# Attention on one core: where turned row maxima and diagonal masks stand in a hand-written order

## The chip, the cores and the metric

The kernel runs on one core of one Trainium2 chip. The metric is device time in microseconds from start to end of one execution. Three executions of the kernel before took 2019.26, 2020.14 and 2020.37 us; the median is 2020.14 us.

## What is computed

A transformer layer on 2048 tokens of width 512: a layer norm, causal attention with 16 heads of 32, and a gated feed-forward part, both added to the input.

```python
xn = _layernorm(x, axis=-1)
# attention
qkv = jnp.einsum('bsh,oh->bso', hidden_states, w_qkv)   # 16 heads of 32
scores = jnp.einsum('bhqd,bhkd->bhqk', q, k) * scale
scores = jnp.where(causal, scores, jnp.finfo(scores.dtype).min)
probs = jax.nn.softmax(scores, axis=-1)
attn = jnp.einsum('bhqk,bhkd->bhqd', probs, v)
# feed-forward
gelu = jnp.tanh(0.7978845608028654 * (gate + 0.044715 * gate ** 3)) * gate * 0.5 + gate * 0.5
inter = gelu * up
x = x + attn @ w_o.T + inter @ Wd.T
```

## The kernel before, in words

Three stages follow each other: `norm_and_project` (norm, q, k and v to scratch memory), `attention`, and `project_and_feed_forward`. The change touches `attention` alone.

Attention handles the heads in 8 pairs (`PAIRS`). For a pair there are two kinds of scores. The **units** (`scores`, L680) are query-major: 128 queries by up to 512 keys into one of four banks of `p_s`; they serve only to find each query's maximum. VectorE reduces each unit to one column of `max_part` (L604, or L600 with the mask added where the unit touches the diagonal). When all units of a chunk of 512 queries are reduced, `join_parts` (L611) joins them, GpSimd splits the maxima into three bf16 parts (`split`, L504 to L514), and TensorE **turns** them: `turn_max` (L690) multiplies `max_cols` by an identity and puts the maxima as rows into a bank of `p_s`. ScalarE copies that bank into spare rows of `q_stack` (`max_row`, L540). There they take part in the second kind of scores, so that the maximum is already subtracted when these come out. Each head of a chunk has one turned maximum: 64 in all, for 8 pairs, 4 chunks and 2 heads.

The **scores_t** (L706) are key-major: 128 keys by up to 512 queries into one of three banks of `p_st`. On the diagonal a second matmul, `mask_k` by the identity (L712, 128 columns, bf16), adds the mask into the same bank. ScalarE takes the exponential into `e_sb` (`exps`, L551), and the **products** (`product_v`, L727) multiply it by v into `p_o`, with a row of sums. `copy_out` (L562) takes `p_o` to SBUF when a chunk is done.

A step is one block of 128 keys of one chunk; a pair has 40 steps (chunks of 4, 8, 12 and 16), and the last four of each chunk are its diagonal. Every step has two pieces, one per head. The order of the work is written out by hand in groups of 4 steps (`GS`), numbered by `k` from 0 to 79: group `k` issues the eight pieces of scores_t of the next group's steps (`LEAD` = 4), the units that `units_of(k)` assigns to it in eight parts (`some_units`), and the products of its own four steps. Since the chunks are multiples of four steps, a group's scores_t are all on the diagonal or none is. Eight units is the normal measure; the first groups take up to `UNITS_FIRST` = 12, until they are `UNITS_AHEAD` = 56 ahead.

`TURNS[k]` lists the turned maxima of group `k`. For pairs 1 to 7 they are turned one group before the scores_t that need them (`TURN_LEAD` = 1), for the last two chunks of pair 0 in the same group (`FIRST_LEAD` = 0); those of chunks 0 and 1 of pair 0 come before group 0. `ring` (L327) is the order in which units and turned maxima take the four banks of `p_s`, and `bank_free` (L665) waits for the reader of the bank's former content: VectorE for a unit, ScalarE's `max_row` for a turned maximum.

TensorE opens a group so:

```python
for t in TURNS[k]:
    turn_max(*t)
for n in range(3):
    scores_t(x + n)
some_units(0, 8)
some_units(1, 8)
scores_t(x + 3)
```

and closes it with `scores_t(x + 7)`, four `product_v` and `some_units(7, 8)`. ScalarE takes in a group three exps, the copies of the turned maxima, `copy_out` of a finished chunk, and five exps (L573 to L585); for pair 0 the copies come first.

Of the kernel before, what the change touches and what calls it, by code (L numbers as in the profile page):

```python
# [29 lines left out]
P = 128  # L30
# [232 lines left out]
def attention(nc, qk_scratch, v_scratch, sum_scratch, rsum_scratch, wo_t, wo_sb, attn_t):  # L263
# [14 lines left out]
    UNITS_FIRST = 12  # L278
    UNITS_AHEAD = 56
    TURN_LEAD = 1  # L280
    FIRST_LEAD = 0
# [22 lines left out]
    for k in range(NG):  # L304
        done = min(NUNIT, max(done + UNITS_GROUP, min(done + UNITS_FIRST, UNITS_GROUP * (k + 1) + UNITS_AHEAD)))
        unit_end.append(done)

    def units_of(k):
        return list(range(unit_end[k - 1] if k else FIRST, unit_end[k]))
# [4 lines left out]
    for p in range(PAIRS):  # L314
        for r in range(TC):
            last = p * NU + UNITS_TO[r]
            BATCHES[-1 if last <= FIRST else next(k for k in range(NG) if unit_end[k] >= last)].append((p, r))
            wanted = (p * NS + CHUNK_START[r] - LEAD) // GS
            for a in range(2):
                TURNS[max(-1, -1 if p == 0 and r < 2 else wanted - (FIRST_LEAD if p == 0 else TURN_LEAD))].append((p, r, a))  # L320
# [7 lines left out]
    for k in range(NG):  # L328
        ring += TURNS[k] + units_of(k)
# [6 lines left out]
    with ExitStack() as ctx:  # L336
# [200 lines left out]
        def _(act):  # L537
# [35 lines left out]
            for k in range(NG):  # L573
                x = (GS * k + LEAD) * PIECES
                for t in TURNS[k]:
                    if t[0] == 0:
                        max_row(*t)
                for n in range(3):
                    exps(x + n)
                for t in TURNS[k]:  # L580
                    if t[0] > 0:
                        max_row(*t)
                copy_out_before(k)
                for n in range(3, GS * PIECES):
                    exps(x + n)  # L585

        @block.vector
        def _(dve):
# [62 lines left out]
            for k in range(NG):  # L651
# [5 lines left out]
                for p_, r in BATCHES[k]:  # L657
                    join_parts(p_, r)
# [5 lines left out]
        def _(pe):  # L664
# [29 lines left out]
            def scores_t(x):  # L694

                g, heads = piece(x)
# [4 lines left out]
                if kt == 0:  # L701
                    pe.wait_ge(max_rows, turn_index[p, qc, heads[-1]] + 1)
                if x >= ST_BUFS:
                    pe.wait_ge(exp_done, x - ST_BUFS + 1)
                for n, a in enumerate(heads):
                    last = nc.tensor.matmul(p_st[:, x % ST_BUFS, n, 0:W - q0],  # L706
                                            k_stack[p % PB][a][:, kt * P:(kt + 1) * P],
                                            q_stack[p % PB][a][:, qc * W + q0:(qc + 1) * W], start=True,
                                            stop=not DIAG[s])
                if DIAG[s]:  # L710
                    for n, a in enumerate(heads):
                        last = nc.tensor.matmul(p_st[:, x % ST_BUFS, n, 0:P], ident[:, :], mask_k[:, :], start=False,  # L712
                                                stop=True)
                last.then_inc(st_ready, 1)
# [23 lines left out]
            for x in range(LEAD * PIECES):  # L738
                scores_t(x)
            pe.wait_ge(o_cleared, 1)  # L740
            for k in range(NG):
# [6 lines left out]

                for t in TURNS[k]:
                    turn_max(*t)  # L750
                for n in range(3):
                    scores_t(x + n)
                some_units(0, 8)
                some_units(1, 8)
                scores_t(x + 3)
                some_units(2, 8)
                scores_t(x + 4)
                some_units(3, 8)
                scores_t(x + 5)
                some_units(4, 8)  # L760
                some_units(5, 8)
                scores_t(x + 6)
                some_units(6, 8)
                scores_t(x + 7)
# [395 lines left out]
```

## Time and profile before

| | us |
|---|---|
| median of three runs | 2020.14 |
| the profiled execution, its own time | 2020.79 |
| span of its profile | 2018.9 |
| TensorE matmuls busy | 1882.5 (93% of the span) |
| VectorE busy | 1090.2 (54%) |
| ScalarE busy | 693.9 (34%) |
| GpSimd busy | 310.7 (15%) |
| mean granted TensorE clock | 0.984 of full speed |

The profile gives for each engine the time in which it worked; matmuls are pipelined and their ends are modelled, so that a busy TensorE can still be waiting a little between matmuls, and the starts tell more than the durations. PE is TensorE's matmuls, PEld its weight loads, DVE is VectorE, ACT ScalarE, POOL GpSimd. L706 is line 706 of the kernel. "idle 0.86 <-ACT q_stack L540" says that an engine stood still for 0.86 us and that ACT's instruction of line 540 released it.

### The profile page before, as it was taken

How to read it: one execution, taken by the hardware profiler on the slowest of the kernel's cores; microseconds unless marked ns; L12 is line 12 of the kernel's file. 1: busy time of each engine (PE TensorE's matmuls, PEld its weight loads, DVE VectorE, ACT ScalarE, POOL GpSimd, SP SyncE). 2: the span in 40 equal slices, each digit the busy share in tenths (PEclk: the TensorE clock that was granted, in tenths of full speed). 3: DMA queues.
4: the chain of work that ended last, by engine and by line, in shares of the span. 5: the costliest groups of instructions: out<-in, count | busy, mean ns of one | idle time of the engine just before them, and what ended most of it. 6: DMA issues, size and time to landing. Idle time of an engine off the chain costs nothing.

```text
span 2018.9 us, 23894 instructions
## 1 busy us (share of the span) xinstructions
PE 1882.5 (93%) x8448; PEld 1325.6 (66%) x8448; DVE 1090.2 (54%) x1706; ACT 693.9 (34%) x1112; POOL 310.7 (15%) x339
## 2 busy tenths in 40 slices
PE   2997799999999999989999999999999999999998
PEld 2785444444444444336787778777877787778776
DVE  7220566565565655643565556555655565556553
ACT  2221345455555555511222222222222222222231
POOL 0002200100101111101212221222122212221221
PEclk9999699999999999999999999999999999999999
DMA  3654603223134040052100110111011101110002
GB/s 146 237 190 119 124 6 79 62 49 81 40 69 82 17 93 6 11 198 63 32 7 26 31 31 5 27 31 31 2 29 31 31 1 30 31 31 0 0 1 83
DMA packets 88857, 109.31 MB, mean 54 GB/s; under 512 B 44248, under 2 KB 60632, under 8 KB 85008
## 3 DMA queue, kind: packets, MB, share of 16 engines
q1 hardware_dynamic: 88784, 108.39, 19.9%
q8 instruction: 40, 0.66, 0.1%
q14 instruction: 33, 0.27, 0.1%
HBM read 75.09 MB, written 29.59 MB: 52 GB/s over the span
## 4 chain that ended last, share of the span: by engine, by line
DVE 21%; ACT 12%; POOL 10%; issue 7%; PE 6%; POOLq 0%; DVEq 0%; ACTq 0%
POOL poly L958 7%; DVE acc L1031 5%; DVE inter L1011 4%; DVE inter L1015 4%; ACT inter L930 3%; POOL poly L955 3%; ACT gate L926 3%; ACT poly L927 3%; DVE weight L1000 3%; ACT i_hi L933 2%; DVE magnitude L994 2%; DVE pair L987 2%; PE p_out L1096 1%; DVE high L991 1%; PE p_gate L1096 1%
## 5 line engine op out<-in xcount | busy, mean ns | idle before, releaser
L551 ACT ACTIVATE e_sb<-p_st 128x512 f32<-128x512 f32 (+3 forms) x640 | 297.3, 548 | 279.8 <-PE p_st L706 145.8
L604 DVE TENSOR_REDUCE max_part<-p_s 128x1 f32<-128x512 f32 x384 | 241.7, 684 | 108.7 <-PE p_s L680 108.5
L680 PE MATMUL p_s<-k_stack,q_stack 96*128 96x512 f32 (+3 forms) x640 | 232.8, 413 | 42.8 <-ACT q_stack L540 21.0
L1011 DVE SCALAR_TENSOR_TENSOR inter<-inter,gate 128x1024 f32<-128x1024 f32 x64 | 78.5, 1226 | 329.7 <-ACT inter L930 329.7
L727 PE MATMUL p_o<-e_sb,v_stack 128*33 128x512 f32 (+5 forms) x1280 | 251.0, 535 | 0.0
L706 PE MATMUL p_st<-q_stack,k_stack 128*128 128x512 f32 (+3 forms) x640 | 235.0, 405 | 6.7 <-ACT e_sb L551 5.0
L48 PE MATMUL p_up<-xn_hi,w_hi 128*128 128x512 f32 x512 | 201.0, 393 | 25.3 <-DVE inter L1015 25.3
L955 POOL TENSOR_SCALAR poly<-poly 128x1024 f32<-128x1024 f32 x64 | 67.4, 1053 | 938.8 <-ACT poly L927 938.8
L600 DVE CUSTOM_DVE_ANT_0 masked_scores<-p_s,score_mask 128x128 f32<-128x128 f32 (+3 forms) x256 | 119.7, 487 | 158.0 <-PE p_s L680 157.0
L48 PE MATMUL p_out<-i_hi,w_hi 128*128 128x512 f32 x512 | 200.0, 391 | 3.1 <-DVE acc L1031 3.1
L48 PE MATMUL p_gate<-xn_hi,w_hi 128*128 128x512 f32 x512 | 201.6, 394 | 0.5 <-ACT poly L927 0.5
L50 PE MATMUL p_out<-i_hi,w_lo 128*128 128x512 f32 x512 | 199.8, 390 | 0.0
L49 PE MATMUL p_out<-i_lo,w_hi 128*128 128x512 f32 x512 | 199.7, 390 | 0.0
L49 PE MATMUL p_gate<-xn_lo,w_hi 128*128 128x512 f32 x512 | 199.4, 389 | 0.0
L50 PE MATMUL p_gate<-xn_hi,w_lo 128*128 128x512 f32 x512 | 199.4, 389 | 0.0
L49 PE MATMUL p_up<-xn_lo,w_hi 128*128 128x512 f32 x512 | 199.3, 389 | 0.0
L50 PE MATMUL p_up<-xn_hi,w_lo 128*128 128x512 f32 x512 | 199.3, 389 | 0.0
L680 PEld LDWEIGHTS p_s<-k_stack,q_stack 96*128 96x128 f32 x640 | 120.6, 197 | 111.4 <-issue 55.7
L920 ACT ACTIVATE w_hi<-weight 128x1024 fp32r<-128x1024 f32 x48 | 50.9, 1061 | 390.7 <-DVE weight L1000 390.7
L727 PEld LDWEIGHTS p_o<-e_sb,v_stack 128*33 128x33 f32 (+1 forms) x1280 | 70.7, 114 | 146.2 <-issue 108.1
L706 PEld LDWEIGHTS p_st<-q_stack,k_stack 128*128 128x128 f32 x640 | 122.5, 194 | 59.2 <-ACT e_sb L551 45.2
L958 POOL TENSOR_TENSOR poly<-poly,gate 128x1024 f32<-128x1024 f32 x64 | 153.4, 2396 | 5.3
(103 smaller groups left out, 2590.7 us busy)
## 6 DMA issues: line engine op xcount, KB each, us to landing
q_stack<-qk_scratch SPq DMA_DIRECT2D x48, 256.0 KB, 7.2
k_stack<-qk_scratch SPq DMA_DIRECT2D x48, 256.0 KB, 8.3
qk_scratch<-out_hi SPq DMA_DIRECT2D x32, 256.0 KB, 2.6
qk_scratch<-out_lo SPq DMA_DIRECT2D x32, 256.0 KB, 3.3
scales<-in_gate_up_s SPq DMA_DIRECT2D x128, 64.0 KB, 2.3
x_sb<-in_x SPq DMA_DIRECT2D x4, 1024.0 KB, 11.8
xn_lo_scratch<-xn_lo_made SPq DMA_DIRECT2D x1, 4096.0 KB, 13.3
v_scratch<-out_v SPq DMA_DIRECT2D x16, 256.0 KB, 2.0
```

Of the source, the lines that this page charges most:

```text
L48: nc.tensor.matmul(out, w_hi, x_hi, start=first, stop=False)
L49: nc.tensor.matmul(out, w_hi, x_lo, start=False, stop=False)
L50: return nc.tensor.matmul(out, w_lo, x_hi, start=False, stop=last)
L551: nc.scalar.activation(e_sb[:, x % E_BUFS, :, 0:w], p_st[:, x % ST_BUFS, :, 0:w], ACT.Exp, scale=SCALE).then_inc(exp_done, 1)
L600: nc.vector.tensor_tensor_reduce(out=masked_scores[:, m % 2, 0:w], in0=p_s[:, slot[n] % S_BUFS, 0:w], in1=score_mask[:, W - w:], scale=1.0 ...
L604: nc.vector.reduce_max(part, p_s[:, slot[n] % S_BUFS, 0:w], AX.X).then_inc(maxed, 1)
L680: nc.tensor.matmul(p_s[:, slot[n] % S_BUFS, 0:w], q_stack[p % PB][a][0:ROWS, i * P:(i + 1) * P], k_stack[p % PB][a][0:ROWS, b * W:b * W + ...
L706: last = nc.tensor.matmul(p_st[:, x % ST_BUFS, n, 0:W - q0], k_stack[p % PB][a][:, kt * P:(kt + 1) * P], q_stack[p % PB][a][:, qc * W + q0 ...
L727: last = nc.tensor.matmul(p_o[a * VW:a * VW + width, q0:], v_stack[p % PB][:, kt, a, 0:width], e_sb[:, x % E_BUFS, a if PH == 2 else 0, 0: ...
L955: nc.gpsimd.tensor_scalar(poly[:, :, :], poly[:, :, :], GELU_A, 1.0, ALU.mult, ALU.add).then_inc(poly_done, 1)
L958: nc.gpsimd.tensor_tensor(poly[:, :, :], poly[:, :, :], gate[:, :, :], ALU.mult).then_inc(poly_done, 1)
L1011: nc.vector.scalar_tensor_tensor(inter[:, :, :], inter[:, :, :], 1.0, gate[:, :, :], ALU.add, ALU.mult).then_inc(gelu_done, 1)
```

## The change

Five things are edited, and each pair's arithmetic stays the same.

- On TensorE the turned maxima of a group move from its head to a place behind its eight scores_t and seven eighths of its units, ahead of the products. The ring of banks is written to match.
- On ScalarE the copies of the turned maxima come after the group's eight exps.
- In a diagonal group the scores_t of both heads of a step come first, and then both masks; the units are placed between these pairs of pieces. In the other groups the order of scores_t and units is as before.
- The turned maxima of pair 0 also come one group ahead (`FIRST_LEAD` goes), and group 0 takes up to 20 units instead of 12, so that they are ready.
- On VectorE `join_parts` follows directly behind the last unit that it needs.

```diff
-    UNITS_FIRST = 12
+    UNITS_FIRST = (20, 12)
...
-    FIRST_LEAD = 0
...
-        done = min(NUNIT, max(done + UNITS_GROUP, min(done + UNITS_FIRST, UNITS_GROUP * (k + 1) + UNITS_AHEAD)))
+        done = min(NUNIT, max(done + UNITS_GROUP, min(done + UNITS_FIRST[min(k, 1)], UNITS_GROUP * (k + 1) + UNITS_AHEAD)))
...
-                TURNS[max(-1, -1 if p == 0 and r < 2 else wanted - (FIRST_LEAD if p == 0 else TURN_LEAD))].append((p, r, a))
+                TURNS[max(-1, -1 if p == 0 and r < 2 else wanted - TURN_LEAD)].append((p, r, a))
...
-        ring += TURNS[k] + units_of(k)
+        units = units_of(k)
+        ring += units[:7 * len(units) // 8] + TURNS[k] + units[7 * len(units) // 8:]
...
                 x = (GS * k + LEAD) * PIECES
-                for t in TURNS[k]:
-                    if t[0] == 0:
-                        max_row(*t)
                 for n in range(3):
                     exps(x + n)
-                for t in TURNS[k]:
-                    if t[0] > 0:
-                        max_row(*t)
                 copy_out_before(k)
                 for n in range(3, GS * PIECES):
                     exps(x + n)
+                for t in TURNS[k]:
+                    max_row(*t)
...
-                for p_, r in BATCHES[k]:
-                    join_parts(p_, r)
+                    for p_, r in BATCHES[k]:
+                        if n + 1 == p_ * NU + UNITS_TO[r]:
+                            join_parts(p_, r)
...
+            def mask_t(x):
+
+                if piece(x)[0] < NSTEP:
+                    nc.tensor.matmul(p_st[:, x % ST_BUFS, 0, 0:P], ident[:, :], mask_k[:, :], start=False,
+                                     stop=True).then_inc(st_ready, 1)
...
-            for x in range(LEAD * PIECES):
+            for x in range(0, LEAD * PIECES, 2):
                 scores_t(x)
+                scores_t(x + 1)
+                mask_t(x)
+                mask_t(x + 1)
...
+                if DIAG[(GS * k + LEAD) % NS]:
+                    for n in (0, 2, 4, 6):
+                        scores_t(x + n)
+                        scores_t(x + n + 1)
+                        mask_t(x + n)
+                        mask_t(x + n + 1)
+                        for part in {0: (0, 1, 2), 2: (3,), 4: (4, 5), 6: (6,)}[n]:
+                            some_units(part, 8)
+                else:
+                    for n in range(GS * PIECES):
+                        scores_t(x + n)
+                        for part in {2: (0, 1), 3: (2,), 4: (3,), 5: (4, 5), 6: (6,)}.get(n, ()):
+                            some_units(part, 8)
                 for t in TURNS[k]:
                     turn_max(*t)
-                for n in range(3):
-                    scores_t(x + n)
-                some_units(0, 8)
-                some_units(1, 8)
-                scores_t(x + 3)
...
-                scores_t(x + 7)
                 for g in range(GS * k, GS * k + GS):
                     product_v(g)
                 some_units(7, 8)
```

Two places show what the instructions do. The first is TensorE in group 18, in the middle of attention, from the last unit of the group before. Before, the head of the group read so (p_s are units, or turned maxima where they come from `max_cols`; p_st are scores_t, or masks where they come from `mask_k`):

```order
L680 MATMUL p_s<-k_stack,q_stack 128x512 [waits maxed]
L690 MATMUL p_s<-ident_bf,max_cols 32x128 [waits maxed,max_split]
L690 MATMUL p_s<-ident_bf,max_cols 32x128 x3
L690 MATMUL p_s<-ident_bf,max_cols 32x128 [waits maxed,max_split]
L690 MATMUL p_s<-ident_bf,max_cols 32x128 x3
L706 MATMUL p_st<-q_stack,k_stack 128x512 [waits exp_done]
L712 MATMUL p_st<-mask_k,ident_bf 128x128
L706 MATMUL p_st<-q_stack,k_stack 128x512 [waits exp_done]
L712 MATMUL p_st<-mask_k,ident_bf 128x128
L706 MATMUL p_st<-q_stack,k_stack 128x384 [waits exp_done]
L712 MATMUL p_st<-mask_k,ident_bf 128x128
L680 MATMUL p_s<-k_stack,q_stack 128x384 [waits maxed] x2
```

Now the end of the same group reads so:

```order
L702 MATMUL p_st<-q_stack,k_stack 128x256 [waits exp_done] x2
L711 MATMUL p_st<-mask_k,ident_bf 128x128 x2
L677 MATMUL p_s<-k_stack,q_stack 128x512 [waits maxed] x2
L702 MATMUL p_st<-q_stack,k_stack 128x128 [waits exp_done] x2
L711 MATMUL p_st<-mask_k,ident_bf 128x128 x2
L677 MATMUL p_s<-k_stack,q_stack 128x512 [waits maxed]
L687 MATMUL p_s<-ident_bf,max_cols 32x128 [waits maxed,max_split]
L687 MATMUL p_s<-ident_bf,max_cols 32x128 x3
L687 MATMUL p_s<-ident_bf,max_cols 32x128 [waits maxed,max_split]
L687 MATMUL p_s<-ident_bf,max_cols 32x128 x3
L725 MATMUL p_o<-e_sb,v_stack 33x512 [waits exp_done]
```

The turned maxima went from ahead of the first score to between the last unit and the first product, and masks stand in pairs. The second place is ScalarE in group 11, which also has a `copy_out`. Before:

```order
L551 ACTIVATE e_sb<-p_st 128x384 [waits pv_done,st_ready]
L540 ACTIVATE q_stack<-p_s 32x512 [waits max_turned] x2
L562 ACTIVATE o_sb<-p_o 97x512 [waits o_stored0,pv_done]
L551 ACTIVATE e_sb<-p_st 128x384 [waits pv_done,st_ready]
L551 ACTIVATE e_sb<-p_st 128x256 [waits pv_done,st_ready] x2
L551 ACTIVATE e_sb<-p_st 128x128 [waits pv_done,st_ready] x2
```

Now:

```order
L551 ACTIVATE e_sb<-p_st 128x384 [waits pv_done,st_ready]
L562 ACTIVATE o_sb<-p_o 97x512 [waits o_stored0,pv_done]
L551 ACTIVATE e_sb<-p_st 128x384 [waits pv_done,st_ready]
L551 ACTIVATE e_sb<-p_st 128x256 [waits pv_done,st_ready] x2
L551 ACTIVATE e_sb<-p_st 128x128 [waits pv_done,st_ready] x2
L540 ACTIVATE q_stack<-p_s 32x512 [waits max_turned] x2
```

The two copies went from behind the third exp to behind the eighth. Now every group that turns maxima is one whose scores_t are on the diagonal.

## Rows read from the trace of the kernel before

**Rows 1.** Windows: length, busy us of each engine (instructions), clock, DMA.
```profile
193.00:228.00 35.00, 17.81 (x58) 11.86 (x59) 11.95 (x42) 6.74 (x14) 18.68 (x21) 0.50 1.03 201
228.00:868.60 640.60, 603.38 (x3015) 302.78 (x3014) 377.14 (x906) 338.13 (x723) 68.29 (x178) 0.99 0.23 49
868.60:2018.90 1150.30, 1112.14 (x4736) 888.72 (x4736) 639.82 (x651) 304.13 (x304) 220.79 (x128) 0.99 0.11 33
```

**Rows 2.** Waits of PE, 300 to 868 us: total us, times, longest.
```profile
PE p_s L680 <- ACT q_stack L540: 21.0, 27, 0.9
PE p_st L706 <- ACT e_sb L551: 4.4, 13, 1.2
PE p_s L680 <- DVE max_part L604: 0.2, 1, 0.2
```

**Rows 3.** Timeline of PE, one turn group: start, us, operation, idle before.
```profile
386.67 0.49 PE L680 MATMUL p_s<-k_stack,q_stack 96*128 96x512 f32 x1
387.09 0.62 PE L690 MATMUL p_s<-ident_bf,max_cols 128*32 128x128 bf16 x8
387.64 0.51 PE L706 MATMUL p_st<-q_stack,k_stack 128*128 128x512 f32 x1
387.99 0.23 PE L712 MATMUL p_st<-mask_k,ident_bf 128*128 128x128 bf16 x1
388.03 0.48 PE L706 MATMUL p_st<-q_stack,k_stack 128*128 128x512 f32 x1
...
390.39 0.50 PE L680 MATMUL p_s<-k_stack,q_stack 96*128 96x512 f32 x1 [0.86 <-ACT q_stack L540]
...
392.56 3.63 PE L727 MATMUL p_o<-e_sb,v_stack 128*33 128x512 f32 x16
396.11 0.51 PE L680 MATMUL p_s<-k_stack,q_stack 96*128 96x512 f32 x1
```

**Rows 4.** Timeline of ACT in the same group.
```profile
388.25 1.47 ACT L551 ACTIVATE e_sb<-p_st 128x512 f32<-128x512 f32 x3 [4.34 <-PE p_st L712]
389.75 1.07 ACT L540 ACTIVATE q_stack<-p_s 32x512 fp32r<-32x512 f32 x2
```

**Rows 5.** Timeline of PE in the first pair, groups 1 and 2.
```profile
241.29 3.63 PE L727 MATMUL p_o<-e_sb,v_stack 128*33 128x512 f32 x16
...
248.38 1.03 PE L690 MATMUL p_s<-ident_bf,max_cols 128*32 128x128 bf16 x8 [2.80 <-POOL max_cols L514]
...
249.67 1.71 PE L706 MATMUL p_st<-q_stack,k_stack 128*128 128x512 f32 x3 [0.25 <-ACT q_stack L540]
...
256.39 2.35 PE L727 MATMUL p_o<-e_sb,v_stack 128*33 128x512 f32 x16
```

**Rows 6.** Windows: the first stretch at the lower clock.
```profile
247.38:254.20 6.82, 5.57 (x19) 4.24 (x20) 2.36 (x4) 3.48 (x7) 0.74 (x4) 0.50 0.00 0
```

**Rows 7.** Timeline of DVE and PE in group 0.
```profile
229.23 2.48 DVE L604 TENSOR_REDUCE max_part<-p_s 128x1 f32<-128x512 f32 x4 [9.53 <-PE p_s L680]
...
232.05 2.48 DVE L604 TENSOR_REDUCE max_part<-p_s 128x1 f32<-128x512 f32 x4
...
233.15 2.35 PE L727 MATMUL p_o<-e_sb,v_stack 128*33 128x512 f32 x16
```

**Rows 8.** Three scores in a row (timeline), and their weight loads (lines by form).
```profile
371.59 0.87 PE L706 MATMUL p_st<-q_stack,k_stack 128*128 128x512 f32 x3
...
L706 PEld LDWEIGHTS p_st<-q_stack,k_stack 128*128 128x128 f32 x640 | 122.5, 194 | 59.2 <-ACT e_sb L551 45.2 <-issue 2.8 <-ACT q_stack L540 1.6
```

**Rows 9.** Timeline of PE: starts of products in groups 4 to 7.
```profile
274.00 3.63 PE L727 MATMUL p_o<-e_sb,v_stack 128*33 128x512 f32 x16
...
287.70 2.35 PE L727 MATMUL p_o<-e_sb,v_stack 128*33 128x512 f32 x16
...
295.62 3.63 PE L727 MATMUL p_o<-e_sb,v_stack 128*33 128x512 f32 x16
...
304.62 3.63 PE L727 MATMUL p_o<-e_sb,v_stack 128*33 128x512 f32 x16
```

More of the change, by code:

```diff
@@ L694, in scores_t @@
             def scores_t(x):
-                g, heads = piece(x)
+                g, (a,) = piece(x)
                 if g >= NSTEP:
@@ L701, in scores_t @@
                 if kt == 0:
-                    pe.wait_ge(max_rows, turn_index[p, qc, heads[-1]] + 1)
+                    pe.wait_ge(max_rows, turn_index[p, qc, a] + 1)
                 if x >= ST_BUFS:
                     pe.wait_ge(exp_done, x - ST_BUFS + 1)
[L705 to L714, printed above, removed]
+                last = nc.tensor.matmul(p_st[:, x % ST_BUFS, 0, 0:W - q0], k_stack[p % PB][a][:, kt * P:(kt + 1) * P],
+                                        q_stack[p % PB][a][:, qc * W + q0:(qc + 1) * W], start=True,
+                                        stop=not DIAG[s])
+                if not DIAG[s]:
+                    last.then_inc(st_ready, 1)
+            def mask_t(x):
+                if piece(x)[0] < NSTEP:
+                    nc.tensor.matmul(p_st[:, x % ST_BUFS, 0, 0:P], ident[:, :], mask_k[:, :], start=False,
+                                     stop=True).then_inc(st_ready, 1)
             def product_v(g):
@@ L747, in some_units @@
                         scores(n)
+                if DIAG[(GS * k + LEAD) % NS]:
[11 more added lines that the diff above has]
+                            some_units(part, 8)
                 for t in TURNS[k]:
                     turn_max(*t)
-                for n in range(3):
-                    scores_t(x + n)
-                some_units(0, 8)
-                some_units(1, 8)
-                scores_t(x + 3)
[L756 to L763, printed above, removed]
-                scores_t(x + 7)
                 for g in range(GS * k, GS * k + GS):
```

## The prediction

> **What bounds the kernel now.** The views were read in this order: the windows by stage, the table of waits of the matmul engine (PE), the timeline of one group in the middle of attention, and the timeline of the first pair of heads.
>
> The windows [rows 1] show the stage that the change touches, attention, from 228.0 to 868.6 us: PE is busy 603.38 of 640.60 us, VectorE (DVE) 377.14, ScalarE (ACT) 338.13. So PE sets the pace, and only what PE no longer waits for or no longer does can count. The feed-forward stage behind it (1150.30 us) has no edit and starts when attention ends; I cost it at nothing.
>
> The waits after the first pair [rows 2] are nearly one wait: p_s matmuls (L680) wait for ACT's copies of turned maxima (L540) 27 times, 21.0 us in all. DVE holds PE once, for 0.2 us. That makes the wait on ACT the first thing to explain.
>
> The timeline of one such group [rows 3] explains it. PE turns two maxima at 387.09, at the head of the group, into two of the four p_s banks. It issues three scores with their masks, two p_s matmuls, one more score, and stands 0.86 us before the p_s matmul at 390.39, which wants the bank of the first turned maximum. ACT [rows 4] was idle for 4.34 us before 388.25, then has three exps in a row first (1.47 us), and comes to the two copies at 389.75. The wait is not a lack of ACT's time, it is the place of the copies in ACT's order.
>
> The timeline of the first pair [rows 5] shows the same operations in a worse place: there the maxima are joined, split by POOL and turned at the head of the very group whose scores need them. PE is idle 2.80 us before the turn at 248.38. The granted clock is then 0.50 of full speed, the lower of its two levels, from 247.38 to 254.20 [rows 6].
>
> **The change, part by part.** I measure a group from the start of one group's products (L727) to the next's: eight scores_t, eight p_s units (twelve in the first eight groups), four steps of products.
>
> A. Turned maxima of pairs 1 to 7 (28 groups). Removed: the 21.0 us of [rows 2]. What must hold: in the new order PE turns them after the eighth score and seven of the eight units, and then starts the products, which take 396.11 - 392.56 = 3.55 us [rows 3]. ACT at that time has at most the two 128-column exps left, under 0.98 us even at the pitch of 512 columns (three in 1.47 us), and then the two copies, 1.07 us [rows 4]. That ends within 2.1 us of the turn, inside the 3.55 us. Where the products are those of a diagonal, 2.35 us as at 256.39 [rows 5], it still fits. The products need exps of the group before, so they wait for none of this. Queued behind the turn on PE are the products and one unit; the turn waits for DVE to free two banks. DVE needs 2.48 us for four 512-column units [rows 7], 0.62 each. The second turn needs the fifth unit's maximum, some 0.35 + 5 x 0.62 = 3.45 us after the first unit's matmul starts (the 0.35 is an estimate of a matmul and a signal). PE reaches it after five units more at 0.235 us (1.2), six scores of 384, 256 and 128 columns (0.75 in proportion), six masks at 0.11 on average (0.65), 0.42 from the last unit to the first turn and half of the turns' 0.55 [rows 3]: 3.3 us. So that wait is some 0.15 us or nothing, and it has no slack. A = -21.0, ends -24 (the 0.86 us hides part of a pipeline's length, so a stall is a little longer than its idle time) and -10 (half comes back at the banks or at the exps).
>
> B. Masks (128 pairs of them, in 32 groups). Now a score with its mask takes 388.03 - 387.64 = 0.39 us [rows 3]; a 512-column score followed by another takes 0.235 us, from three in 0.87 us with the last one's 0.40 taken off [rows 8]. So a mask costs 0.155 us. A 128-column bf16 matmul right behind another takes 0.07 us: eight turn matmuls between 387.09 and 387.64 [rows 3]. The remaining 0.085 us I read as the next float32 weight load, which a mask of 128 columns is too short to cover. In the new order the second mask follows the first, so one of two such losses goes: 128 x 0.085 = 10.9 us. But a 256 or 128-column score is itself too short a cover for the second head's weight load, so in half of the pairs the loss only moves, and 5.5 us are left. Against it stands a new exposure. The exp of the first head cannot start until both scores are issued, and with three p_st banks the second score of the 256-column pair needs the exp of a head one pair back. By the walk it comes 0.1 us late, in 32 groups: +3.2. B = -2.3, ends -11 and +5.
>
> C. The first pair. Between products 241.29 and 256.39 lie 15.10 us [rows 5], between 274.00 and 287.70 13.70 us, and between 295.62 and 304.62, a group with as many units and no turn, 9.00 us [rows 9]. The excess is 6.1 + 4.7 = 10.8 us, the slower clock included. The turns themselves only move: from the p_s matmul at 386.67 to the p_st matmul at 387.64 is 0.97 us instead of 0.235 [rows 3], 0.74 each, 1.5 for both. So 9.3 us go. The price is the longer group 0, 20 units for 12. Its DVE work starts at 229.23 [rows 7]. PE must issue 17 units ahead of the products, and the 17th wants the bank of the 13th: nine 512-column maxima at 0.62, two of 128 and two of 256 columns (estimated 0.21 and 0.34), 6.7 us, so 235.9, and the products start near 236.4 instead of 233.15. Of the 3.2 us, seven units at 0.235 are only moved, so 1.6 us are lost. In groups 1 and 4 the turns now stand behind ten or more units and wait for DVE: the second turn wants the maxima of two more units than the products want now, 1.24 us, less its own 0.74, some 0.5 us each: 1.0. C = -9.3 + 1.6 + 1.0 = -6.7, ends -9.3 and -3.
>
> D. The join of the maxima directly behind its last unit on DVE: one operation a little earlier, nobody waits for it after the first pair. Nothing. POOL's and SP's instructions and their order are the same.
>
> Sum: -21.0 - 2.3 - 6.7 = -30.0 us against the profiled execution's 2020.79 us (its span is 2018.90, and the 1.89 us around it stay): 1990.8. That execution lies 0.65 us over the median of the three, so I forecast **1990 us**.
>
> One rule speaks against part B. By the trace, 512-column scores follow each other at 0.235 us although each one's weight load is recorded with 194 ns [rows 8]; the sum of the two would be 0.4 us, so the load runs under the matmul before it. The Trainium skill (TensorE: Matmul & The Clock Gate, "Part 3: Packing small matmuls — row/col tiling") says that a weight load overlaps matmuls in flight only when the two use different row groups. All of these use all 128 rows, so by the rule nothing is hidden and pairing masks saves nothing; the trace disagrees with it.
>
> **The rivals.**
> - *The wait comes back elsewhere.* The turn now waits for DVE's fifth maximum with no slack, and all products queue behind it. For it: the walk's 3.45 against 3.3 us. Against: DVE holds PE for 0.2 us now [rows 2]. If half of A returns: 10.5 us more, 2000.5. Chance 0.20.
> - *Pairing masks saves nothing*, because weight loads are not covered in either order, while the exps still come later: the 5.5 us left in B drop out, 1995.5. Chance 0.10. This is what the skill's rule would give.
> - *Group 0 eats the gain of the first pair.* Twenty units in one group leave PE waiting on DVE in pieces, and the granted clock, 0.50 up to 228 us [rows 1], comes up later, or falls again as it did after the idle time of [rows 5, 6]. C goes to zero: 1997. Chance 0.07.
> - *More than forecast*: A at 24, B at 6, C at 9: 2020.1 - 39 = 1981. Chance 0.12.
> - *Slower*: the exps become the chain on the diagonal. In each pair of a diagonal group but the first, the second head's score waits for an exp of the pair before: three places in 32 groups, 96 waits. An exp of 512 columns has a pitch of 0.49 us [rows 4]; if each wait were that long, 47 us come in, against 33.2 us gained elsewhere (the sum without its 3.2 us of late exps): about 2034. It decides beyond 0.35 us a wait. For it: PE already waits 13 times for exps, 4.4 us [rows 2]. Against: units stand between the pairs, and ACT is idle before each burst [rows 4]. Chance 0.05.
> - The change does what it says: the order of PE's instructions is changed in every diagonal group, so there is no chance kept for "nothing moved".
>
> **How the numbers follow.** The forecast with its own range, 1984 to 1997, has 0.46. The range given runs from 1980, which takes in most of "more than forecast", to 2005, which takes in the half-returned wait. About 0.2 lies outside. What a measurement of this kernel can tell from no change is some 0.2%, 4 us. Faster by more than that: all but the slower rival and a sliver, 0.93. Within: 0.02. Slower: 0.05.
>
> **What would show it.** In the profile after: no wait of p_s on ACT's copies after the first pair, or some 1 us of it; the turn between a p_s matmul and the first product; no idle time near 248 and 280 us and the clock at full speed there; a p_s wait on DVE of 1 to 3 us in group 0; the stretch that is now 5.89 us, from the p_s matmul at 386.67 to the products at 392.56 [rows 3], some 0.85 us shorter. The forecast is wrong if waits of the turn on DVE, or of p_st on exps, sum to over 10 us, or if attention's stretch is less than 20 us shorter.

## The result, and the profile after

The changed kernel takes 1987.72 us (median) against 2019.70 us of the kernel before on the same chip: ratio 0.9844, 95% interval 0.9827 to 0.9860, or 31.5 us less by that ratio (the medians lie 32.0 us apart). One of the four executions behind the changed kernel's median took 3921.14 us, is counted as slow and is not in the ratio; the other three took 1987.22 to 1988.05 us. The forecast was 1990 us with a range of 1980 to 2005.

The windows of the changed kernel, divided where the feed-forward stage begins to run (length, busy us of PE, PEld, DVE, ACT and POOL, clock, DMA):

```profile
228.00:838.82 610.82, 593.68 (x3015) 300.73 (x3013) 375.24 (x908) 335.44 (x723) 68.27 (x178) 0.99 0.24 50
838.82:1986.20 1147.38, 1111.22 (x4736) 888.56 (x4736) 638.23 (x648) 304.12 (x304) 220.63 (x128) 1.00 0.11 33
```

Attention's stretch went from 640.6 us to 610.8 [rows 1], but the two windows do not end at the same event. The first matmul of the feed-forward stage, before and then after:

```profile
870.84 2.90 PE L1096 MATMUL p_gate<-acc,wo_sb 128*128 128x512 f32 x3 [5.46 <-PEq L336]
```

```profile
838.97 2.90 PE L1096 MATMUL p_gate<-acc,wo_sb 128*128 128x512 f32 x3 [5.46 <-PEq L336]
```

The window of [rows 1] ends at 868.60, 2.24 us ahead of it. Counted from 228.00 us to this matmul, attention went from 642.8 us to 611.0, 31.9 us less; the feed-forward stage, which has no edit, is 0.9 us shorter. PE's busy time in attention fell by 9.7 us only; the rest of the 31.9 us was idle time. What is left of PE's waits from 300 us on is one line, against three [rows 2]:

```profile
PE p_st L702 <- ACT e_sb L551: 6.2, 24, 0.5
```

The wait on ACT's copies, 21.0 us before, is gone, and nothing on DVE took its place. Waits for exps grew from 4.4 to 6.2 us, from 13 places to 24. Group 18, whose head is [rows 3], now reads on PE:

```profile
375.30 0.50 PE L677 MATMUL p_s<-k_stack,q_stack 96*128 96x512 f32 x1
375.64 0.63 PE L702 MATMUL p_st<-q_stack,k_stack 128*128 128x512 f32 x2
376.12 0.28 PE L711 MATMUL p_st<-mask_k,ident_bf 128*128 128x128 bf16 x2
376.21 0.82 PE L677 MATMUL p_s<-k_stack,q_stack 96*128 96x384 f32 x3
376.87 0.60 PE L702 MATMUL p_st<-q_stack,k_stack 128*128 128x384 f32 x2
377.31 0.29 PE L711 MATMUL p_st<-mask_k,ident_bf 128*128 128x128 bf16 x2
377.41 0.48 PE L677 MATMUL p_s<-k_stack,q_stack 96*128 96x512 f32 x1
377.73 0.78 PE L702 MATMUL p_st<-q_stack,k_stack 128*128 128x256 f32 x2
378.35 0.28 PE L711 MATMUL p_st<-mask_k,ident_bf 128*128 128x128 bf16 x2
...
379.22 0.29 PE L711 MATMUL p_st<-mask_k,ident_bf 128*128 128x128 bf16 x2
379.32 0.47 PE L677 MATMUL p_s<-k_stack,q_stack 96*128 96x512 f32 x1
379.72 0.62 PE L687 MATMUL p_s<-ident_bf,max_cols 128*32 128x128 bf16 x8
380.27 3.63 PE L725 MATMUL p_o<-e_sb,v_stack 128*33 128x512 f32 x16
383.83 0.50 PE L677 MATMUL p_s<-k_stack,q_stack 96*128 96x512 f32 x1
```

and on ACT:

```profile
376.38 2.07 ACT L551 ACTIVATE e_sb<-p_st 128x512 f32<-128x512 f32 x4 [3.83 <-PE p_st L711]
378.62 0.66 ACT L551 ACTIVATE e_sb<-p_st 128x256 f32<-128x256 f32 x2 [0.17 <-PE p_st L711]
379.49 0.45 ACT L551 ACTIVATE e_sb<-p_st 128x128 f32<-128x128 f32 x2 [0.22 <-PE p_st L711]
380.16 1.07 ACT L540 ACTIVATE q_stack<-p_s 32x512 fp32r<-32x512 f32 x2 [0.22 <-PE p_s L687]
```

From the p_s matmul ahead of the first score to the first product it is 380.27 - 375.30 = 4.97 us, against 5.89 us before; 5.04 was forecast. The turned maxima stand at 379.72, ahead of the products, and ACT's copies run from 380.16 to 381.23 while PE is in its 3.56 us of products. Two things are new beside this: ACT stands still for 0.17 us before its exps of 256 columns, and the two 256-column scores, from 377.73 to the masks at 378.35, take 0.62 us, although by the pitch of 512-column scores, 0.235 us, two of them would take 0.24.

The first pair, starts of products on PE in groups 0 to 2:

```profile
236.44 2.35 PE L725 MATMUL p_o<-e_sb,v_stack 128*33 128x512 f32 x16
...
246.44 3.63 PE L725 MATMUL p_o<-e_sb,v_stack 128*33 128x512 f32 x16
...
255.85 2.35 PE L725 MATMUL p_o<-e_sb,v_stack 128*33 128x512 f32 x16
```

Group 0's products start at 236.44, where 236.4 had been worked out. That the two agree to 0.1 us is in part luck: the clock stood at its lower level until 234.7 us in this profile and until 230.3 us in the one before, and in the profiles of e2, e5, e7, e9, e10, e11 and e12, with as many units in group 0, the products start between 235.1 and 236.5. The wait of p_s on DVE in group 0, 1 to 3 us by the forecast, does not show. Groups 1 and 2 lie 9.41 us apart instead of 15.10 [rows 5], and the clock stays at its upper level:

```profile
236.00:260.00 24.00, 22.75 (x115) 11.85 (x116) 17.39 (x41) 10.67 (x23) 1.07 (x5) 1.00 0.03 6
```

### The profile page after: what moved, and what is told of

The parts are those of the page before. It is cut to its first block, busy times and chain, and to the rows that moved or that the text cites. A ratio compares the mean times of both kernels' runs of the same rounds, so it can differ in the third digit from the quotient of the medians.

```text
span 1986.2 us, 23894 instructions
## 1 busy us (share of the span) xinstructions
PE 1871.4 (94%) x8448; PEld 1322.6 (67%) x8448; DVE 1086.7 (55%) x1706; ACT 691.5 (35%) x1112; POOL 310.6 (16%) x339
## 4 chain that ended last, share of the span: by engine, by line
DVE 22%; ACT 12%; POOL 10%; issue 7%; PE 6%; POOLq 0%; DVEq 0%; ACTq 0%
POOL poly L958 7%; DVE acc L1031 5%; DVE inter L1011 4%; DVE inter L1015 4%; ACT inter L930 3%; POOL poly L955 3%; ACT gate L926 3%; ACT poly L927 3%; DVE weight L1000 3%; ACT i_hi L933 2%; DVE magnitude L994 2%; DVE pair L987 2%; PE p_out L1096 1%; DVE high L991 1%; PE p_gate L1096 1%
## 5 line engine op out<-in xcount | busy, mean ns | idle before, releaser
L677 PE MATMUL p_s<-k_stack,q_stack 96*128 96x512 f32 (+3 forms) x640 | 225.9, 408 | 21.6 <-DMA k_stack<-qk_scratch 19.6
L702 PE MATMUL p_st<-q_stack,k_stack 128*128 128x512 f32 (+3 forms) x640 | 226.9, 402 | 10.8 <-ACT e_sb L551 7.4
```

The lines of the kernel that those rows point to most:

```text
L677: nc.tensor.matmul(p_s[:, slot[n] % S_BUFS, 0:w], q_stack[p % PB][a][0:ROWS, i * P:(i + 1) * P], k_stack[p % PB][a][0:ROWS, b * W:b * W + ...
L702: last = nc.tensor.matmul(p_st[:, x % ST_BUFS, 0, 0:W - q0], k_stack[p % PB][a][:, kt * P:(kt + 1) * P], q_stack[p % PB][a][:, qc * W + q0 ...
```

## The experiments

All times are medians; each ratio is to the kernel before on the same chip. To compare kernels in the same place, the table gives besides the stretch from the first product of group 10 to that of group 70 (24 turn groups, the clock at its upper level throughout), read from the timelines. Each stretch is of one profile; where two kernels have the same code in it (the change and e3, e2 and e6) the stretches agree to 0.1 us.

| kernel | us | ratio, 95% interval | groups 10 to 70, us |
|---|---|---|---|
| before | 2018 to 2020 | | 469.6 |
| changed | 1987.72 | 0.9844 (0.9827 to 0.9860) | 449.6 |
| e1 turns alone | 1997.52 | 0.9895 (0.9879 to 0.9912) | 451.4 |
| e2 masks apart | 1984.34 | 0.9831 (0.9814 to 0.9847) | 446.2 |
| e3 first pair as before | 1994.87 | 0.9881 (0.9865 to 0.9898) | 449.6 |
| e4 copies first | 1995.33 | 0.9884 (0.9867 to 0.9900) | 450.0 |
| e5 e2 with old unit places | 1989.43 | 0.9857 (0.9842 to 0.9872) | 451.4 |
| e6 e2 with 16 units | 1985.56 | 0.9836 (0.9823 to 0.9850) | 446.1 |
| e7 e2 with wide masks | 1984.08 | 0.9828 (0.9815 to 0.9842) | 446.8 |
| e8 e2, turn behind all units | 2001.01 | 0.9917 (0.9903 to 0.9930) | 457.2 |
| e9 pairs in the first step | 1981.39 | 0.9818 (0.9805 to 0.9832) | 444.7 |
| e10 pairs in the later steps | 1988.12 | 0.9852 (0.9837 to 0.9868) | 450.1 |
| e11 e2, last units earlier | 1982.89 | 0.9825 (0.9811 to 0.9838) | 445.9 |
| e12 pairs in the second step | 1985.92 | 0.9844 (0.9830 to 0.9857) | 448.7 |

**e1: only the turned maxima move.** To the kernel before:

```diff
-                for t in TURNS[k]:
+                for t in [t for t in TURNS[k] if t[0] == 0]:
                     turn_max(*t)
...
                 scores_t(x + 7)
+                for t in [t for t in TURNS[k] if t[0] > 0]:
+                    turn_max(*t)
```

with ring and copies to match.

> The kernel before, with the turned maxima of pairs 1 to 7 moved behind the eighth score and their copies behind the eighth exp; masks and the first pair stay as before. Theory (the wait came from the place of the copies and goes entirely): 21 us less, 1998.7 us, no wait of p_s on ACT's copies after the first pair. Rival (the turn now waits for DVE, or p_st for exps): half of it comes back, 2009 us, with over 8 us of such waits. If term A was undersized because idle time hides part of a stall: 1995 to 1996 us.

Measured: 1997.52 us, 21.6 us less than the kernel before. The wait on the copies is gone, and PE's waits in that profile show what the lack of slack costs (in this kernel L692 is the turn and L606 DVE's reduction ahead of it, L708 is the scores' matmul and L553 the exps):

```profile
PE p_s L692 <- DVE max_part L606: 5.7, 28, 0.2
PE p_st L708 <- ACT e_sb L553: 3.2, 12, 0.5
```

28 turns wait 0.2 us each for DVE. Term A holds.

**e2: each mask behind its own score again.** To the changed kernel:

```diff
                         scores_t(x + n)
-                        scores_t(x + n + 1)
                         mask_t(x + n)
+                        scores_t(x + n + 1)
                         mask_t(x + n + 1)
```

> The changed kernel with each mask directly behind its own score again, units and turns at their new places. Theory (a mask of 128 columns is too short to cover the next float32 weight load; pairing saves one of two such losses for wide scores, less some late exps): 2 to 4 us slower than the change, 1990 to 1992 us. Rival (weight loads are not covered in either order): the same or up to 3 us faster, 1984.5 to 1987.7 us.

Measured: 1984.34 us, 3.4 us *faster* than the change, just below the rival's range, and so the sign of my term B is wrong: pairing the masks costs time. The two ratios' intervals overlap a little, but the stretch of groups 10 to 70 says the same, 446.2 against 449.6 us.

**e3: the first pair as before.** The changed kernel with `UNITS_FIRST = (12, 12)` and, for pair 0, the turn at the head of the group that needs it and the copies ahead of the exps. The join of the maxima stays at its new place on DVE, directly behind the last unit that it needs, and the units and masks of the diagonal groups stay where the change has them.

> The changed kernel with the first pair's turned maxima at the head of the group that needs them, their copies ahead of the exps, and 12 units in group 0. Theory: the two stops near 248 and 280 us come back with their stretches at half clock, and group 0's products start 3.3 us earlier: 6.7 to 7.8 us slower than the change, 1994.4 to 1995.5 us. Rival (the long group 0 gives most of it back later): under 3 us slower, 1990 us.

Measured: 1994.87 us, 7.2 us slower than the change; groups 10 to 70 are the same to 0.1 us. In the two profiles group 8's products start 4.5 us apart, at 309.8 and 305.3, and the last product 6.1 us apart. The other 1.6 us lie in the last group of products, which in e3's profile ran at the lower clock (from 832.5 us). So what e3 puts back is worth 4.5 us in the first pair, and I can't say whether the clock at the end of attention goes with the edit or is chance. Of the two stops that were to come back only one did, that of [rows 5]:

```profile
PE p_s L692 <- POOL max_cols L515: 2.8, 1, 2.8
```

The second stop, near 280 us in the kernel before, is absent, and with it the stretch at the lower clock. The join of chunk 3's maxima on DVE and the turn on PE, before:

```profile
278.68 0.18 DVE L611 TENSOR_REDUCE row_max<-max_part 128x8 f32<-128x32 f32 x1
280.33 0.62 PE L690 MATMUL p_s<-ident_bf,max_cols 128*32 128x128 bf16 x8 [2.27 <-POOL max_cols L514]
```

and in e3:

```profile
274.21 0.19 DVE L612 TENSOR_REDUCE row_max<-max_part 128x8 f32<-128x32 f32 x1
277.32 0.62 PE L692 MATMUL p_s<-ident_bf,max_cols 128*32 128x128 bf16 x8
```

Before, the join stood behind units that PE issued only after the products; in e3 it runs 4.5 us earlier and the turn waits for nothing. This is term D, which I had put at nothing. e3 reaches group 8's products 3.8 us before e1, which has the whole first pair as before, join included (309.81 against 313.65 us). No run moves the join alone; e3 differs from e1 also in the places of units and masks.

**e4: one edit to the kernel before.**

```diff
                 for t in TURNS[k]:
-                    if t[0] == 0:
-                        max_row(*t)
+                    max_row(*t)
                 for n in range(3):
                     exps(x + n)
-                for t in TURNS[k]:
-                    if t[0] > 0:
-                        max_row(*t)
```

> The kernel before with one edit: ScalarE copies the turned maxima of all pairs ahead of the group's three exps instead of behind them. Theory (the wait is the place of the copies in ACT's order, not ACT's time): the 21.0 us wait on the copies goes; the exps start some 0.6 us later, so p_st waits for exps grow by 0.2 to 0.3 us in 28 groups; net 13 to 16 us less, 2004 to 2007 us. Rival (what matters is ACT's total work at that point): the wait only changes its name, 2018 to 2021 us.

Measured: 1995.33 us, 23.8 us less: more than the theory gave, and more than e1's large move on PE. The loss by later exps did not come. ACT's timeline of group 18:

```profile
382.63 1.07 ACT L540 ACTIVATE q_stack<-p_s 32x512 fp32r<-32x512 f32 x2 [3.62 <-PE p_s L686]
383.73 2.54 ACT L551 ACTIVATE e_sb<-p_st 128x512 f32<-128x512 f32 x6
386.54 0.70 ACT L551 ACTIVATE e_sb<-p_st 128x128 f32<-128x128 f32 x2 [0.26 <-PE p_st L708]
```

The copies run 1.07 us, and then six exps go in one train of 2.54 us, with no idle time between them; before, ACT had 1.47 us of exps, the copies, and more exps that waited for scores which PE could not issue. PE waits for exps 3.6 us in all, less than in the kernel before. The price of exps that start 0.6 us later, 0.2 to 0.3 us a group, was wrong: ACT catches up. Moving the turn on PE as well, as e1 and the change do, is thus not what removes the wait, and e1's turns wait 5.7 us for DVE where e4's wait for nothing. No run has e4's order of TensorE's and ScalarE's work together with the change's first pair and places of units.

**e5: e2 with the units where they stood before.** In a diagonal group the units follow the third, fourth, fifth, sixth and seventh piece, as in the other groups, instead of standing between the steps.

> The kernel of e2 (masks apart) with one edit: in diagonal groups the units stand between the scores where they stood before (two after the third piece, and so on) instead of three behind the first pair. Theory (the new places send DVE its units earlier, and without them the turned maxima wait for DVE as in e1, 28 times 0.2 us): 5 to 7 us slower than e2, 1989.3 to 1991.3 us, with some 5.7 us of waits of the turn on DVE. Rival (e2 is faster for the masks alone, the places of units are worth nothing): 1984 to 1985 us.

Measured: 1989.43 us, 5.1 us slower than e2; the intervals overlap a little, but the stretch of groups 10 to 70 is 5.2 us longer. That stretch is 451.4 us as in e1: from there on the two differ in the place of the join alone, which is worth nothing after the first pair. In the first pair they differ by the change's whole treatment of it, join included, and e5 is 8.1 us faster than e1. The turn's waits on DVE are e1's too, and they are 7 times and 1.5 us in e2:

```profile
PE p_s L687 <- DVE max_part L600: 5.7, 28, 0.2
PE p_st L702 <- ACT e_sb L551: 3.2, 12, 0.5
```

The places of the units are thus a part of the change with a worth of its own, 5 us, and I had given it no term.

**e6: 16 units in group 0**, `UNITS_FIRST = (16, 12)` in e2.

> The kernel of e2 with 16 units in group 0 instead of 20. Theory (group 0 is bound by DVE, 0.62 us for a unit of 512 columns against 0.235 on PE, so four units fewer make its stop shorter, and the later groups have room for them): group 0's products start 1.5 to 2.5 us earlier, the time falls by 0.5 to 1.5 us, 1982.8 to 1983.8 us. Rival (DVE's work is only moved to groups 1 to 7, which are as full): the same, 1984.3 us.

Measured: 1985.56 us, 1.2 us slower than e2, with intervals that overlap. Products of group 0 start at the same 235.3 us in both profiles, but in e6's the clock was at the lower level from 244.2 to 251.0 us and in e2's from 234.7 to 238.1 us, so the first pairs can't be compared to a microsecond. The theory failed: nothing is gained and the products start no earlier. In its place e6's profile has a wait that e2's has not: with 16 units the maxima are split too late for the turn of group 1, which waits 2.34 us for POOL at 245.66 us. Group 10's products start 4.2 us later than in e2, in a profile of e6's slowest execution (1987.09 us).

**e7: masks of 256 columns** in e2, with zeros in the added half. `rest2` shares the memory of `rest1` to make room.

```diff
-                    nc.tensor.matmul(p_st[:, x % ST_BUFS, 0, 0:P], ident[:, :], mask_k[:, :], start=False,
+                    w = min(2 * P, W - STEPS[piece(x)[0] % NS][2])
+                    nc.tensor.matmul(p_st[:, x % ST_BUFS, 0, 0:w], ident[:, :], mask_k[:, 0:w], start=False,
```

> The kernel of e2 with masks of 256 columns instead of 128 where the piece has room (192 of 256 masks); the extra columns add zero. Theory (a mask's cost behind its score is the next float32 weight load, which 53 ns of columns don't cover): the 128 extra columns run under that load and cost nothing, 1984 to 1986 us. Rival (the cost of a mask is its own and fixed): 192 x 0.053 = 10 us slower than e2, 1994 us.

Measured: 1984.08 us, the same as e2 (1984.34). 192 masks stream twice the columns (the lines by form, with the number, busy us and mean ns of one):

```profile
L712 PE MATMUL p_st<-mask_k,ident_bf 128*128 128x256 bf16 x186 | 52.5, 283 | 0.0
L712 PE MATMUL p_st<-mask_k,ident_bf 128*128 128x128 bf16 x62 | 13.4, 232 | 0.0
```

and the kernel is no slower; its stretch of groups 10 to 70 is 0.6 us longer, where the added columns of that stretch's 144 wide masks alone would take 8 us (the turn's eight matmuls of 128 bf16 columns follow each other at 0.056 us). So the added columns of a mask that stands between two float32 matmuls are nearly free up to 256. This fits the reading on which term B's price rested, that what is paid there is the load of the next weights. It does not show it: any cost of a mask that is longer than its columns would look the same.

**e8: the turned maxima behind all units** of the group in e2.

```diff
+                some_units(7, 8)
                 for t in TURNS[k]:
                     turn_max(*t)
                 for g in range(GS * k, GS * k + GS):
                     product_v(g)
-                some_units(7, 8)
```

> The kernel of e2 with the turned maxima behind all of the group's units instead of seven eighths of them, still ahead of the products. Theory (the turn has just no slack against DVE): each turn wants the maximum of one more unit, 0.62 us, against 0.235 us more of PE's work, so some 0.3 to 0.4 us of new waiting on DVE in 28 groups: 8 to 11 us slower than e2, 1992 to 1995 us. Rival (there is slack): 1984 to 1985 us.

Measured: 2001.01 us, 16.7 us slower than e2 and above the theory's range. The turn's waits on DVE are 8.3 us, and the stretch of groups 10 to 70 is 11.0 us longer, 0.46 us for each of its 24 turn groups. (Another 6 us are lost before group 10, most of it in the first pair, where the groups have twelve units.) The slack is less than one unit: a single unit more ahead of the turn already costs this.

**e9, e10 and e12: which pairs cost.** e2 with a pair of masks in some steps of the diagonal group: the first (512 columns), the other three, the second alone (384).

```diff
-                        mask_t(x + n)
-                        scores_t(x + n + 1)
+                        if n == 0:
+                            scores_t(x + n + 1)
+                            mask_t(x + n)
+                        else:
+                            mask_t(x + n)
+                            scores_t(x + n + 1)
```

(`n != 0` in e10, `n == 2` in e12.)

> The kernel of e2 with the masks paired in the first step of a diagonal group only (the 512-column one). Theory (pairing costs by the chain of exps: the first exp starts 0.3 us later, and the second score of the 256-column step waits that much longer for it; PE itself gains 0.05 us on the pair): 2 to 6 us slower than e2, with the waits of p_st on exps at the changed kernel's level (5.4 us of idle time). Rival (pairing costs on PE itself, in the narrow steps): within 1 us of e2, or 1.6 us faster.

> The kernel of e2 with the masks paired in the other three steps and apart in the first. Theory (as e9: the chain's start is not delayed, PE loses 0.03 to 0.05 us in the narrow pairs): 0 to 4 us slower than e2, less than e9, waits of p_st on exps near e2's 3.2 us. Rival: the whole 3.4 us of pairing stand here.

Measured: e9 1981.39 us, 3.0 us faster than e2, and e10 1988.12, 3.8 us slower. For e9 the intervals overlap; its stretch of groups 10 to 70 is 1.5 us shorter than e2's, and e10's 3.9 longer. My theory fell: a late first exp costs nothing that shows, and the pair of 512-column scores is a gain of those 1.5 us. The rival that the loss stands in the later steps is right. In the traces of e10 and of the change ACT stands still before its third or fifth exp. Thus a new theory, and e12:

> The kernel of e2 with the masks paired in the second step of a diagonal group alone (the 384-column one). Theory after e9 and e10 (pairing there delays the first head's mask, so ACT stands still before its third exp, and the second 256-column score, which needs that exp's bank, waits): the whole loss of pairing stands here, 4 to 6 us slower than e2 in the groups after the first pair, 1987 to 1989 us, with an idle gap of ACT before its third exp and waits of p_st on exps of 5 us. Rival (the loss stands in the two narrow steps, on PE itself): within 1 us of e2, 1983.5 to 1985 us.

Measured: 1985.92 us, 1.6 us slower than e2 and outside both ranges; the stretch of groups 10 to 70 is 2.5 us longer (3.9 in e10). So some two thirds of the loss of the later steps stand in the second, the rest in the last two. How it arises, group 14 of e2 on PE, from the 384-column scores on:

```profile
346.84 0.39 PE L702 MATMUL p_st<-q_stack,k_stack 128*128 128x384 f32 x1
347.07 0.23 PE L711 MATMUL p_st<-mask_k,ident_bf 128*128 128x128 bf16 x1
347.11 0.42 PE L702 MATMUL p_st<-q_stack,k_stack 128*128 128x384 f32 x1
347.37 0.23 PE L711 MATMUL p_st<-mask_k,ident_bf 128*128 128x128 bf16 x1
347.41 0.31 PE L677 MATMUL p_s<-k_stack,q_stack 96*128 96x128 f32 x1
347.56 0.33 PE L702 MATMUL p_st<-q_stack,k_stack 128*128 128x256 f32 x1
347.73 0.23 PE L711 MATMUL p_st<-mask_k,ident_bf 128*128 128x128 bf16 x1
347.88 0.38 PE L702 MATMUL p_st<-q_stack,k_stack 128*128 128x256 f32 x1
```

and of e12:

```profile
346.26 0.56 PE L702 MATMUL p_st<-q_stack,k_stack 128*128 128x384 f32 x2
346.66 0.29 PE L711 MATMUL p_st<-mask_k,ident_bf 128*128 128x128 bf16 x2
346.76 0.31 PE L677 MATMUL p_s<-k_stack,q_stack 96*128 96x128 f32 x1
346.90 0.33 PE L702 MATMUL p_st<-q_stack,k_stack 128*128 128x256 f32 x1
347.07 0.23 PE L711 MATMUL p_st<-mask_k,ident_bf 128*128 128x128 bf16 x1
347.47 0.38 PE L702 MATMUL p_st<-q_stack,k_stack 128*128 128x256 f32 x1 [0.17 <-ACT e_sb L551]
```

The two scores with their masks take no longer as a pair: 347.41 - 346.84 = 0.57 us in e2, 346.76 - 346.26 = 0.50 in e12. But the first of the two masks, which lets ACT begin, stands 0.23 us behind the first score in e2 and 0.40 in e12. ACT in e2, then in e12:

```profile
346.10 2.66 ACT L551 ACTIVATE e_sb<-p_st 128x512 f32<-128x512 f32 x6 [3.42 <-PE p_st L711]
```

```profile
345.52 1.09 ACT L551 ACTIVATE e_sb<-p_st 128x512 f32<-128x512 f32 x2 [3.42 <-PE p_st L711]
346.93 1.43 ACT L551 ACTIVATE e_sb<-p_st 128x384 f32<-128x384 f32 x4 [0.32 <-PE p_st L711]
```

In e2 six exps run nearly in one train (the row hides 0.15 us of idle time before the third, which starts at 347.34). In e12 ACT has done two and stands still for 0.32 us before the third, and the later ones are late with it, by 0.17 us: from the first 384-column score to the third exp it is 346.93 - 346.26 = 0.67 us, against 347.34 - 346.84 = 0.50 in e2. The second 256-column score needs the bank of that third exp: it starts 0.32 us behind the first one in e2 and 0.57 us in e12.

**e11: the last units earlier.** e2 with `4: (4, 5, 6), 6: ()` in place of `4: (4, 5), 6: (6,)`.

> The kernel of e2 with the seventh eighth of a diagonal group's units ahead of the last step's scores instead of behind them, so that DVE has them 0.3 us earlier before the turn. Theory (the turn still waits 7 times, 1.5 us, for DVE in e2): 1 to 2 us faster, 1982.3 to 1983.3 us. Rival (the last scores and so the last exps come later and the copies with them, or the unit's bank is not yet free): 0 to 2 us slower.

Measured: 1982.89 us, intervals overlapping e2's. The stretch of groups 10 to 70 is 0.3 us shorter, and the turn waits for DVE as often as in e2. Inconclusive: the time lies in the theory's range, but the waits that it was to remove stayed, and the two profiles, 1.1 us apart, differ by 0.35 us ahead of group 10 and by 0.6 us in the feed-forward stage, which has no edit.

The fastest kernel of the study is e9, the change with pairs of masks only where the scores have 512 columns: 1981.39 us, 6 us below the change by the medians and 5 by the ratios; their intervals (0.9805 to 0.9832 and 0.9827 to 0.9860) overlap a little.

## Why the prediction was right

- **What bounds the kernel.** Right: PE sets the pace of attention, and 22.2 of the 31.9 us that attention lost were PE's idle time.
- **Term A**, -21.0 us for the turned maxima of pairs 1 to 7. Right: e1 gives -21.6. The walk that found no slack against DVE is borne out by e1 (28 waits of 0.2 us) and by e8; in the change itself no turn after the first pair waits for DVE. (The six scores in it come to 0.70 us in proportion, not 0.75.) "The wait comes back elsewhere" (chance 0.20) did not happen. The reading that the wait came from the place of the copies in ACT's order, and not from ACT's time, is shown by e4, which moves nothing on PE.
- **Term B**, -2.3 us for pairing the masks. Wrong in sign: it costs 3.4 us (e2). The step that failed is "By the walk it comes 0.1 us late, in 32 groups: +3.2". The place was right, the second score of the 256-column pair; the size was not. It comes 0.25 us later (e12 against e2), because ACT has run out of work before the third exp, and the later narrow steps add to it. The other half, 0.085 us a pair for a covered weight load, fits the 512-column step, where e9 gains 1.5 us in 24 groups, 0.06 each, and the 384-column step on PE alone (0.50 us for the pair in e12, 0.57 in e2), where the late exp outweighs it. It is smaller than counted: 0.06 us in 32 groups is 2.0 us where 5.5 had been taken, and the other three steps lose 4.0 us in 24 groups (e10), some 5.3 in all 32; the two make the 3.4. The rival "pairing masks saves nothing" had nearly the measured figure for this term, +3.2, but its mechanism does not fit: e9 has a gain from pairing, and 0.235 us from one 512-column score to the next leaves no room for a load of 0.194 us that is not covered. The rule of the Trainium skill (TensorE: Matmul & The Clock Gate, "Part 3: Packing small matmuls — row/col tiling"), that a weight load overlaps a matmul only across row groups, does not hold for these matmuls, which use all rows. (The same section also lets a load run ahead when it goes to the background weight buffer; no run here tells where a load went.)
- **Term C**, -6.7 us for the first pair. e3 gives 7.2, of which its profile places 4.5 us in the first pair, and the start of group 0's products came as worked out. The mechanism, turning one group ahead, is borne out for the first stop. The second stop, 4.7 us of the excess, I also put down to the place of the turn, and e3's rows show it gone with the turn at its old place.
- **Term D**, the join, put at nothing. After the first pair that is right (e1 and e5: 451.4 us both). In the first pair the earlier join goes with the end of the second stop. C and D together are e5 against e1, 8.1 us; how they share it is open.
- **A term that was missing**: the units of a diagonal group stand between its steps, three of them ahead of the second step. I walked the new order to find the slack of the turn and never asked what the old places would have cost. They are worth 5.1 us (e5), of which the turn's waits for DVE show 4.2 (5.7 us in e1, which has the old places, 1.5 in e2).
- **The sum.** -21.6 (A), -7.2 (C), -5.1 (unit places) and +3.4 (pairs) make -30.5 us against the measured -31.5. With e5 against e1, -8.1, in place of -7.2 they make -31.4, but by construction: those four steps lead from the kernel before over e1, e5 and e2 to the change. My sum of -30.0 came close because the missing gain and the wrong sign of B nearly cancel, 5.1 against 5.7 us: two errors that the total doesn't show. That the total came out to some 2 us is luck; that term A did is not.
- **The slower rival**, the exps as the chain on the diagonal, exists as a mechanism, mostly in one place of a group instead of three and at a quarter of a microsecond.

## What to carry to other kernels

When an engine waits for another that has just been idle, look at the order of the second one's queue before its load: here one edit of ScalarE's order, with TensorE untouched, gave 24 us, as much as moving the work on both. Where a short chain of buffers feeds a consumer, the signal that releases the consumer should be issued as early as possible; grouping like operations delays it, and paid here only in the first step of a group (e9), behind which three units stand ahead of the next scores. Something that is costed at nothing "after the first pair" needs a price in the first pair too. A change of several parts needs one term for each part that moves, places of filler work included, or the total can be right for the wrong reasons.

## What was not expected of the hardware

A mask of 256 columns costs no more than one of 128 when it stands between float32 matmuls whose weights have all 128 columns: 192 of them twice as wide changed the time by -0.3 us, where their added columns alone would be 192 x 0.056, some 10 us. And stretches of 3.4 or 6.8 us at the lower clock come at places that differ from kernel to kernel: at 832.5 us in e3, whose code there is the change's, which has none ahead of 838.8 us; at 807.9 us in e7, where PE had been busy for 7.19 of the 7.90 us before. In e3 the last group of products took 7.50 us instead of 5.81 with 3.4 us at the lower level, so such a stretch moves a time by 1.7 or 3.4 us, which sets a floor to what such comparisons tell.
